# Starting the sixteen attention items of a batch over eleven steps, and finishing them in five, in a two-layer graph kernel

## The reference, cut to what matters

```
h  = relu(layernorm(x))
x  = x + relu([h, max of h over each node's first 25 neighbours] @ W0 + b0)      # layer 0
h  = relu(layernorm(x)) @ W1                                                     # layer 1
s1, s2 = h @ a1, h @ a2
e  = where(adj > 0, leaky_relu(s1[i] + s2[j], 0.4), -1e20)
x  = x + gelu(softmax(e, axis=i) @ h)                                            # for each row block j of h
```

## Time and profile before

| | |
|---|---|
| three timed runs | 4237.78, 4251.37, 4252.88 us; median 4251.37 |
| the profiled execution | 4247.52 us |
| its span on the core | 4245.7 us |
| busy PE, PEld, DVE, ACT, POOL | 2663.3, 1981.0, 3343.1, 2008.2, 3066.7 us |
| gathers | 3200, from 32.1 us to 4093.6 us |
| mean granted clock of TensorE | 0.72 of full speed |

### The profile page before, as it was taken

One profiled execution on the slowest core, in us unless ns is written; L12 is line 12 of the kernel. 1 busy time (PEld: TensorE's weight loads), 2 busy tenths in 40 slices (PEclk: granted clock), 3 DMA queues, 4 the chain that ended last, 5 costly groups with the idle time before them and its releaser, 6 DMA issues. The chain is left out here.

```text
span 4245.7 us, 44096 instructions
## 1 busy us (share of the span) xinstructions
PE 2663.3 (63%) x13568; PEld 1981.0 (47%) x13568; DVE 3343.1 (79%) x7214; ACT 2008.2 (47%) x2704; POOL 3066.7 (72%) x3205
## 2 busy tenths in 40 slices
PE   2434446676666756676666666667666676667669
PEld 2222234455444544454544554445444455445558
DVE  5666679966898769986799867997689966898666
ACT  4222246632566326652366424663356632665236
POOL 5777777777777777777777777777777777777740
PEclk9555557777777776767767777777777777777789
DMA  6555556666666665767666666666666666665641
GB/s 213 170 156 184 175 180 213 215 220 206 213 220 209 227 220 191 223 212 228 216 194 216 224 226 196 221 208 224 224 211 214 216 222 205 216 218 193 192 145 49
DMA packets 412785, 860.12 MB, mean 203 GB/s; under 512 B 67331, under 2 KB 248454, under 8 KB 396166
## 3 DMA queue, kind: packets, MB, share of 16 engines
q0 software_dynamic: 153600, 419.64, 32.4%
q1 hardware_dynamic: 258950, 437.67, 30.5%
HBM read 714.43 MB, written 142.61 MB: 202 GB/s over the span
## 5 line engine op out<-in xcount | busy, mean ns | idle before, releaser
L454 POOL DMA_INDIRECT gb<-h_table,idx x3196 | 3062.2, 958 | 1025.1 <-issue 964.2
L1181 PE MATMUL ps_av<-hz,lk 128*128 128x256 f32 x3584 | 1075.9, 466 | 85.1 <-DVE hz L911 85.1
L828 DVE TENSOR_REDUCE hl<-gb 128x256 f32<-128x3328 f32 x127 | 734.1, 5780 | 366.0 <-DMA gb<-h_table,idx 365.9
L1181 PEld LDWEIGHTS ps_av<-hz,lk 128*128 128x128 f32 x3584 | 847.7, 243 | 308.3 <-issue 153.5
L828 DVE TENSOR_REDUCE gb<-gb 128x256 f32<-128x3328 f32 x128 | 746.6, 5833 | 2.9 <-DMA gb<-h_table,idx 2.9
L1245 PE MATMUL ps_l<-cf,hl 128*128 128x128 f32 x508 | 114.9, 368 | 668.8 <-issue 481.5
L1249 PE MATMUL ps_l<-w,hcat 128*128 128x256 f32 x1016 | 455.7, 625 | 85.7 <-ACT hcat L597 85.7
L597 ACT COPY hcat<-ps_l 128x512 f32<-128x512 f32 x127 | 74.4, 586 | 819.5 <-PE ps_l L1245 819.5
L471 ACT ACTIVATE sg<-ps_c 128x1024 bf16<-128x1024 bf16 x256 | 260.2, 1016 | 337.0 <-PE ps_c L1157 333.9
L1245 PEld LDWEIGHTS ps_l<-cf,hl 128*128 128x128 f32 x508 | 75.1, 185 | 715.1 <-issue 715.1
L1249 PEld LDWEIGHTS ps_l<-w,hcat 128*128 128x128 f32 x1016 | 308.0, 318 | 195.2 <-ACT hcat L597 129.3
(11 more groups left out here) (171 smaller groups left out, 3678.9 us busy)
## 6 DMA issues: line engine op xcount, KB each, us to landing
ad<-in_adj SPq DMA_DIRECT2D x128, 1024.0 KB
p_rest<-lk SPq DMA_DIRECT2D x112, 512.0 KB, 3.5
lk<-p_rest SPq DMA_DIRECT2D x112, 512.0 KB, 4.2
gb<-h_table,idx POOLq DMA_INDIRECT x3196
edges_t<-stage SPq DMA_DIRECT2D x32, 1024.0 KB, 7.0
edge<-edges_t SPq DMA_DIRECT2D x64, 512.0 KB, 7.6
xl<-in_x SPq DMA_DIRECT2D x128, 128.0 KB, 5.9
hl<-h_table SPq DMA_DIRECT2D x128, 128.0 KB, 5.7
```

The costliest lines, as they stand in the source:

```text
L454: pool.indirect_dma_start(gb[c][:, s + (c > 0), :], None, table[tb], bass.IndirectOffsetOnAxis(idx[u][:, k:k + 1], 0)).then_inc(gathered[c ...
L828: V.tensor_reduce(dst, gb[c][:, :, :].rearrange("p k c -> p c k"), AX.X, ALU.max).then_inc(maxed[c], 1)
L1181: ins = T.matmul(ps_av[:, k * C:(k + 1) * C], lk[jj][:, k * P:(k + 1) * P], hz[jj][:, :], start=False, stop=False)
```

## The change

The table `STARTED` spreads the beginnings over steps 0 to 10: two items in steps 0, 2, 4, 6 and 8, one in steps 1, 3, 5, 7, 9 and 10. The items begun in a step are finished for the first sweep (exponential, `av`, store) in the next. The last is done early in step 11. There the accumulators are closed and, late in the same step, opened for the second sweep. The second halves follow two late in step 11, four in each of steps 12, 13 and 14 (two early, two late), one early and one late in step 15. Step 0 then holds no second half of the batch before. ACT's Gelu moves from steps 1 and 9 to steps 0 and 11, in step 11 behind the masks and ahead of `h1t`; DVE's residual add moves from steps 1 and 9 to 1 and 12. Loads of the byte mask (`load_edge`), output stores and residual loads move with them. In the last tile PE has two `av` in place of four.

```
 SP, step
-                if old and before:
-                    load_p(it - 1, 1)
+                if new:
+                    for k in LOADED_EARLY.get(t, ()):
+                        load_p(base + k, k % 2)
                 if n:
...
                     load_xn(m, xn[u][:, :, :], xn_in[u])
...
-                if new and sweep:
-                    load_p(it + 1, 1) if last and t == 15 else load_p(it, 0)
+                if new:
+                    for k in LOADED_LATE.get(t, ()):
+                        load_p(base + k, k % 2)
 ACT, step
-                if fl is not None:
-                    flush(fl)
+                if new and t == 0 and not (b == 1):
+                    flush(b * 2 - 3)
...
                 if a:
                     evacuate_signs(v + 4, (v + 4) % 8 * P, 1)
...
+                if new and t == 11:
+                    flush(b * 2 - 2)
 DVE, step
-                    if not sweep:
-                        item_value(o, it, j, 0)
+                    if now_a is not None:
+                        item_value(o, base + now_a, now_a % 2, 0)
...
-                if new and not sweep:
-                    item_value(o, it + 1, j + 1, 1)
+                if now_b is not None:
+                    item_value(o, base + now_b, now_b % 2, 1)
...
+                if new and v < LAST:
+                    for k in late_items(t):
+                        item_rows(o, base + k, k % 16, k % 2, k // 16)
 PE, step
-                if old:
-                    av(it - 2, 0)
+                if new:
+                    for k in early_items(t):
+                        av(base + k, k % 2)
+                if new and t == 11:
+                    close_sweep()
...
-                if old:
-                    av(it - 1, 1)
-                    if t % 8 == 0:
+                if new and t == 11:
+                    open_sweep(b * 2 - 1)
+                if new:
+                    for k in late_items(t):
+                        av(base + k, k % 2)
+                    if t == 15:
                         close_sweep()
```

More of the change, by code:

```diff
@@ L311, in load_p, with step @@
                 sp.dma_start(lk[jj][:, 0:HALF], p_rest[i % 32 - 16]).then_inc(p_in[jj], 16)
-            def step(b, tb, t, n, a, l, e, w, last, new, old):
+            def step(b, tb, t, n, a, l, last, new):
                 v = b * TILES + t
                 u = t % 2
-                it = (b - 1) * 32 + t * 2
-                sweep, before = t // 8 % 2, (t - 1) // 8 % 2
+                base = (b - 1) * 32
+                before_a, before_b = begun(t - 1, 0), begun(t - 1, 1)
                 if last and t == 15:
@@ L353, in step @@
                         load_l(tb, b, t + 1, (t + 1) % 2)
[L354 to L357 removed]
+                if new and before_a is not None:
+                    store_p(base + before_a, before_a % 2)
+                if new:
+                    for k in LOADED_LATE.get(t, ()):
+                        load_p(base + k, k % 2)
                 if a:
@@ L363, in step @@
                     sp.dma_start(x1_dram[bass.ds(v * P, P), :], x1[u][:, :]).then_inc(x1_stored[u], 16)
-                if old and not before and l:
-                    store_p(it - 1, 1)
+                if new and before_b is not None:
+                    store_p(base + before_b, before_b % 2)
                 if n:
@@ L390, in round_ @@
                     step(b, tb, t, n=0 <= t - N_FIRST < PAIRS and not last, a=not (last and t >= 10),
-                         l=True, e=(t == 15 and not last) or (not first and t < 7),
-                         w=not first and not (b == 1 and t == 0), last=last, new=not first,
-                         old=not first and not (b == 1 and t == 0))
+                         l=True, last=last, new=not first)
                     if not first:
-                        if t == 1 and not (b == 1):
+                        if t == 2 and not (b == 1):
                             store_out(b - 2, 1, b * 2 - 3)
@@ L648, in pair @@
                         t = t0 + u
-                        one = b == 1
-                        fl = {1: b * 2 - 3, 9: b * 2 - 2}.get(t) if not first and not (one and t == 1) else None
                         step(b, i, u, t, n=0 <= t - N_FIRST < PAIRS and not last, a=not (last and t >= 12),
-                             l=True, new=not first, old=not first and not (one and t == 0), fl=fl)
+                             l=True, new=not first)
                 for i in range(PAIRS):
@@ L1128, in pair @@
                         t = t0 + u
-                        one = b == 1
-                        fl = {1: b * 2 - 3, 9: b * 2 - 2}.get(t) if not first and not (one and t == 1) else None
+                        fl = {1: b * 2 - 3, 12: b * 2 - 2}.get(t) if not first and not (b == 1 and t == 1) else None
                         step(o, b, i, u, t, n=0 <= t - N_FIRST < PAIRS and not last,
@@ L1133, in pair @@
                              l=True, g=not (last and t == 15),
-                             new=not first, old=not first and not (one and t == 0), fl=fl)
+                             new=not first, fl=fl)
                     end_order(o)
@@ L1331, in pair @@
                         else:
-                            step(b, i, u, t, a=not (last and t >= 12), l=True, old=not first and not (b == 1 and t == 0))
+                            step(b, i, u, t, a=not (last and t >= 12), l=True, new=not first)
                 for i in range(PAIRS):
```

148 lines of the change are left out of this document (69 added, 79 removed).

## The result

| | before | after |
|---|---|---|
| median of the timed runs, us | 4252.12 (4 runs, 4237.78 to 4253.61) | 4268.65 (4 runs, 4257.86 to 4272.95) |
| ratio of the times | | 1.0041, 95% interval 1.0026 to 1.0057 |
| the profiled execution | 4247.52 | 4257.86 |
| its span | 4245.7 | 4256.1 |
| busy PE / DVE / POOL | 2663 / 3343 / 3067 | 2522 / 3354 / 3075 |

The forecast was 4238, with 4212 to 4268 as its range. The change costs 16.5 us where 13 us of gain were expected. The changed kernel's profiled execution is the fastest of its four, so the two profiles show 10.4 us of these 16.5.

The account below looks back on a forecast made before the run. POOL's gather issue was taken as the bound until the last gather, then PE. Terms -29 (waits) + 2 (step 1) + 13 (step 12) + 0 (PE) + 1 (tail) = -13 us gave a median of 4238 us, range 4212 to 4268.

Parts of the forecast that it names:

- The 29 us should go: In item-beginning steps, POOL's waits for the first-buffer maximum (18 us) and longer gathers behind them (11) vanish: 29 us gained.
- a two-item step costs DVE 32 us, a one-item step 32 - 5 = 27; the mean of two is 29.5: In alternating two-item and one-item steps, DVE's mean step of 29.5 us stays below POOL's 31.3.
- a two-item step uses about 1 of it and the next gives it back: DVE has 3.5 us of room; a two-item step takes about 1 us, which the following step returns.
- Rival 3: Two-item steps still make POOL wait, so only half of the 29 us go: 4251 us, chance 0.16.
- The other 28 us stay: Longer gathers with no wait before them, 28 us of excess, stay because the DVE operations beside them stay: no gain.
- Step 12, 13 us: Row tiles queued on SP behind two `load_p` come late; POOL loses 2.2 us a round in six rounds: 13 us.
- PE's lateness: After step 11's second late `av`, PE reaches the next step's transposes 2.9 us late.
- the landing: In step 12, row tiles take 7.3 us from their issue on SP to their use.
- Steps 12 to 14, PE, nothing: With four second halves a step, PE takes 31 us, neither catching up nor falling back: 0 us.
- rival 2: PE becomes the bound in steps 12 to 14: 4276 us, chance 0.12; sign: transposes over 3.5 us behind the second-buffer maximum.
- Tail, +1: After the last gather: masks about 3 us later behind two late `av`, 2.5 us back elsewhere; +1 us, from -2 to +6.
- -29 + 2 + 13 + 0 + 1 = -13: Whole kernel: waits gone, 2 us kept for step 1's residual add, step 12, PE's steps 12 to 14, tail; 13 us gained.

Follow-up runs that it names:

- b2: The kernel before, run again unchanged for a second profile: ratio 0.9996 to the kernel before.
- a2: The changed kernel, run again unchanged for a second profile: ratio 1.0044 to the kernel before.
- e1: The changed kernel with the row tiles `xn` issued ahead of the early `load_p` on SP: ratio 1.0010 to the kernel before.
- e6: The changed kernel with a plain copy for step 11's Gelu and its two table loads: ratio 1.0018 to the kernel before.
- e8: The changed kernel with the last batch's first two mask loads issued one step earlier: ratio 1.0054 to the kernel before.
- e11: e8 with ACT making the last batch's first four masks ahead of its copy of the half transposes: ratio 1.0036 to the kernel before.
- m1: A separate kernel: 26 gathers in each of seven stretches, beside nothing or one repeated kind of DVE operation; median gather 0.95 us alone, 1.15 to 1.16 beside two-input operations.

## Why the prediction was wrong

- **"The 29 us should go": failed in size.** Between both profiles 12.8 us of waits and 4.0 us behind waits went, 17 of 29; between b2 and a2 only 11. The step that failed is "a two-item step costs DVE 32 us, a one-item step 32 - 5 = 27; the mean of two is 29.5", with "a two-item step uses about 1 of it and the next gives it back". It took DVE's busy time for the step's length and cut it at step boundaries. The trace shows 28.78 us of work in both kinds of step and 31.85 us of mean length, and a DVE that stays 3.0 to 5.6 us behind. The waits before tiles 7 to 9 went all the same. What stayed is mostly one place that the forecast did not have, tile 6 behind the late landing of step 4 (5.3 of 8.2 us). Rival 3 named the outcome (about half stays) but neither cause.
- **"The other 28 us stay": failed in size, and this miss is as large.** The number of DVE operations is the same, but how many of them meet a gather is not. Outside the gathers behind waits the excess went from 29.7 to 42.0 us (b2 to a2: 30.9 to 38.5), a term that the sum put at nothing. Most of it stands beside `val`; that `val` lengthens gathers is shown, why it does so more in this order is open.
- **Step 12, 13 us: right** in mechanism and place, and near in size: 13.3 us here and 19.4 in a2; e1 and e6 took it away from two ends. PE's lateness was put too low (2.9 against 3.3 to 5.6 us) and the landing too long (7.3 against 4.8 to 6.4), and the two nearly cancel.
- **Steps 12 to 14, PE, nothing: right.** PE does not idle before the transposes of steps 12 and 13 and 0.0 to 1.5 us before those of step 14 in rounds 1 to 6. The two early `av` take 7.17 us together (the row of 2492.20), at a granted clock of 1.00, and before the gathers of tile 15 POOL waits 1.3 us in all rounds together. PE's lateness falls from 3.3 to 5.6 us in step 12 to at most 1.9 in step 14. So rival 2's sign, transposes more than 3.5 us late, was there in step 12 in five of six rounds, but its growing lateness was not.
- **Tail, +1: right in the first profile (+1.2), by luck, and too low by the others.** Against b2 a2 shows +6.7. The first profile of the kernel before was one in which its own last maximum came 6.4 us late. The working had the piece "PE reaches the last transposes after two late `av` instead of one, and ACT's first masks stand behind that: about 3 us later"; e8 and e11 together show that it was this piece, and larger, because DVE's last maximum stands behind those masks.
- **The sum.** Forecast: -29 + 2 + 13 + 0 + 1 = -13. Measured in the profiles: -12.8 (waits) + 8.3 (longer gathers) + 13.3 (step 12) + 1.2 (tail) = +10.0, against 10.4 of span. The medians moved by 16.5; of the other 6 us no profile shows the place.

## What to carry to other kernels

A stage's busy time does not say how long it becomes when work is taken out of it: look first for what the freed engine will wait for, here PE at `x<-ps_l` and ACT at the relu, and follow each piece of an item over the step boundary that it crosses. When late work is packed, the fixed duties behind it in a queue (row loads, masks of the next stage) pay; issue or make them ahead of the packed work, and do it in the same change. And where an engine waits behind three things, removing the first only shows the second: e8 gave nothing, and only with e11 did the end get shorter, by 10 us in the profile and 2 to 8 in the times.

## What the runs showed of the hardware

- A gather's issue on POOL took 0.949 us at the median alone, 1.16 beside a 128x512 DVE operation with two SBUF inputs (1.15 beside the add), 1.02 beside the 128x256 scale, and 0.949 beside the 5.7 us maximum and beside an operation with one input in PSUM. Beside a 128x512 operation with one SBUF input the median was 0.950, and 11 of 26 took 1.03 us or more (all m1). The two-input DVE operation beside it took 0.69 us.
- The Trainium skill (SBUF — State Buffer, "SBUF: two separate sides") has the loser of the shared ports blocked for the other's whole instruction, and with two SBUF inputs only against a GpSimd operation that reads SBUF. The m1 trace does not agree: a gather loses 0.21 us there, about a third of one DVE operation, though one or two of them run beside it.
- The earlier trace rows shows a gather of 3.59 us, 2.64 longer than the median, beside four residual adds that take 2.50 us together and the `val` behind them. In m1 no gather beside repeated 512-column adds took longer than 1.153 us. What makes the difference is open.
